# Halves of the values turned between WIV's last pieces, and two relations' counts in one number

## The reference, cut to what matters

```python
# layer 0: attention with two projections in a row for q, k and v
h = relu(layernorm(x))
q, k, v = h @ wq.T + bq, h @ wk.T + bk, h @ wv.T + bv
q2, k2, v2 = q @ wiq.T + biq, k @ wik.T + bik, v @ wiv.T + biv    # 16 heads of 64
scores = q2 @ k2.T / 8 + mask            # mask (96 x 96) from edges and types
x = x + (softmax(scores) @ v2) @ wo.T + bo
# layer 1: relational graph convolution over 1632 edges with 8 relations, and a gate
h = relu(layernorm(x))
u = h @ root + bias
for r in range(8):
    u += (sum of h[src] over the edges of relation r into dst / max(count, 1)) @ weight[r]
z = concat([u, h]) @ w_gate + b_gate
x = x + tanh(u) * z + h * (1 - z)
```

## Time and profile before

| | |
|---|---|
| median of 3 timed runs | 236.71 us (235.92 to 236.77) |
| profiled execution, its own time | 233.02 us |
| its span | 231.5 us |
| TensorE busy | 221.9 us, 96% |
| VectorE busy | 74.7 us, 32% |
| ScalarE busy | 20.1 us, 9% |
| GpSimd busy | 16.2 us, 7% |
| weights read by DMA | 72 fetches of 1024 KB; the queue's packets took 84.3% of 16 engines' span |
| granted TensorE clock | 1.000 over the span |

### The profile page before, as it was taken

One profiled execution on the slowest core, in us unless ns is written; L12 is line 12 of the kernel. 1 busy time (PEld: TensorE's weight loads), 2 busy tenths in 40 slices (PEclk: granted clock), 3 DMA queues, 4 the chain that ended last, 5 costly groups with the idle time before them and its releaser, 6 DMA issues.

```text
span 231.5 us, 10022 instructions
## 1 busy us (share of the span) xinstructions
PE 221.9 (96%) x4829; PEld 213.7 (92%) x4829; DVE 74.7 (32%) x134; ACT 20.1 (9%) x35; POOL 16.2 (7%) x42
## 2 busy tenths in 40 slices
PE   2999999999999999999999999999999999999993
PEld 2889989999999989889998999999999999999993
DVE  2469645231782130525875510000000000000624
ACT  2632000000110120131100000000000000000101
POOL 3260007600000000000000000000000000000000
PEclk9999999999999999999999999999999999999999
DMA  6999999999899866938887779999999998999302
GB/s 230 392 390 420 423 419 420 405 408 396 365 331 392 282 282 218 396 130 335 249 324 238 282 270 395 403 385 384 348 398 395 422 418 337 377 413 396 161 3 71
DMA packets 11275, 77.00 MB, mean 333 GB/s; under 512 B 1466, under 2 KB 1730, under 8 KB 2020
## 3 DMA queue, kind: packets, MB, share of 16 engines
q1 hardware_dynamic: 10704, 75.94, 84.3%
q10 hardware_dynamic: 532, 0.42, 0.6%
HBM read 75.97 MB, written 0.39 MB: 330 GB/s over the span
## 4 chain that ended last, share of the span: by engine, by line
PE 95%; DMA 2%; DVE 1%; issue 1%; ACT 0%
PE acc L728 80%; PE acc L986 3%; PE side L778 2%; PE turn L931 2%; DMA x_sb<-in_x 2%; PE side L931 1%; PE side L986 1%; PE turn L746 1%; PE turn L813 1%; DVE stats L469 1%; PE turn L829 0%; PE side L790 0%; PE side L797 0%; PE turn L790 0%; PE turn L797 0%
## 5 line engine op out<-in xcount | busy, mean ns | idle before, releaser
L728 PE MATMUL acc<-mean,raw 128*64 128x96 f32 x2048 | 85.4, 246 | 0.2
L728 PEld LDWEIGHTS acc<-mean,raw 128*64 128x64 f32 x2048 | 84.8, 137 | 0.9 <-issue 0.8
L728 PE MATMUL acc<-hT,raw 128*64 128x96 f32 x1024 | 44.8, 247 | 0.5 <-issue 0.5
L728 PEld LDWEIGHTS acc<-hT,raw 128*64 128x64 f32 x1024 | 43.1, 137 | 1.9 <-issue 1.5
L691 DVE TENSOR_TENSOR uT<-acc,uT 128x384 f32<-128x384 f32 x2 | 1.1, 558 | 81.9 <-PE acc L728 81.9
L728 PE MATMUL acc<-qT,raw 128*64 128x96 f32 x512 | 22.5, 247 | 0.7 <-issue 0.7
L728 PEld LDWEIGHTS acc<-qT,raw 128*64 128x64 f32 x512 | 21.6, 137 | 1.3 <-issue 1.1
L728 PE MATMUL acc<-kT,raw 128*64 128x96 f32 x512 | 22.3, 247 | 0.0
L728 PEld LDWEIGHTS acc<-kT,raw 128*64 128x64 f32 x512 | 21.4, 137 | 0.8 <-issue 0.7
L728 PE MATMUL acc<-uT,raw 128*64 128x96 f32 x256 | 12.2, 261 | 0.0
L728 PEld LDWEIGHTS acc<-uT,raw 128*64 128x64 f32 x256 | 11.8, 148 | 0.3 <-ACT uT L371 0.2
(11 more groups left out here) (170 smaller groups left out, 149.6 us busy)
## 6 DMA issues: line engine op xcount, KB each, us to landing
raw<-in_weights SPq DMA_DIRECT2D x72, 1024.0 KB, 6.6
x_sb<-in_x ACTq DMA_DIRECT2D x1, 192.0 KB, 3.7
x_sb<-in_x SPq DMA_DIRECT2D x1, 192.0 KB, 3.5
out<-out_rows SPq DMA_DIRECT2D x1, 192.0 KB, 2.1
out<-out_rows ACTq DMA_DIRECT2D x1, 144.0 KB, 2.5
out<-out_rows SPq DMA_DIRECT2D x1, 48.0 KB, 2.2
bias_rows<-in_biases ACTq DMA_DIRECT2D x1, 36.0 KB
edge_i<-in_edge_columns ACTq DMA_DIRECT2D x1, 25.5 KB
```

The lines of the kernel that those rows point to most:

```text
L728: mm = pe.matmul(a[g * HD:(g + 1) * HD, b, c * N:(c + 1) * N], raw[:, s, at:at + HD], moving(k0 + k), start=opens and k0 == 0 and c == 0 a ...
```

## The change

- WIV alone takes its pieces in the order KINDS_WIV = [0, 1, 2, 3]: output half 0 is done after the second piece, half 1 after the fourth. The wait for the second half of qT moves from the third piece to the second.
- `turn_v2(0)` stands between WIV's third and fourth piece, `mix_values(0)` and then `turn_v2(1)` behind the fourth. The transposes go to `acc[0]`, no longer to `turn`; the wait for the second turned half of the attention moves to `mix_values(0)`. ScalarE's order follows: take_v2(0), take_mix(0), take_v2(1), take_mix(1).
- `rel_hot` has 384 columns in place of 768: relations r and r + 4 share a column, and an edge of the upper four counts 2048 instead of 1 (there are 1632 edges). `rel_one_hot` gets a second operation, the multiplication by that step. `count(c)` is one instruction of 384 columns into bank 0 of `side`. No count stands before WO any more: 3 stand between the averages, 13 after them.
- VectorE splits the sums after the sum of squares: it copies them as int32 to `packed`, masks the low 11 bits, and subtracts to get the high part; ScalarE turns both into `counts`, the second with scale 1/2048.
- GpSimd computes the step of each edge and type modulo 4 in three more instructions of 102 x 16, ahead of the ones for the attention's codes. The iota and its copy are half as wide.

The diff, cut to its core:

```diff
+KINDS_WIV = [0, 1, 2, 3]
+PACK = 2048
+def kind_of(n):
+    return (KINDS_WIV if SEQUENCE[n // PIECES] == WIV else KINDS)[n % PIECES]
...
         def done_at(m, b):
-            return first_piece(m) + 3 + b
+            return first_piece(m) + (2 + 2 * b if m == WIV else 3 + b)
...
-            gp.iota(iota_i, [[1, R * N]], base=0, channel_multiplier=0).then_inc(iota_made, 1)
+            gp.iota(iota_i, [[1, TW]], base=0, channel_multiplier=0).then_inc(iota_made, 1)
...
-            step(gp.tensor_scalar(dup_f, type8_f, float(N), None, ALU.mult))
+            step(gp.tensor_scalar(upper_f, type8_f, float(R // 2), float(R // 2), ALU.is_ge, ALU.mult))
+            gp.tensor_scalar(rel_step_f, upper_f, (PACK - 1) / (R // 2), 1.0, ALU.mult, ALU.add).then_inc(edges_ready, 1)
+            step(gp.tensor_tensor(dup_f, type8_f, upper_f, ALU.subtract))
+            step(gp.tensor_scalar(dup_f, dup_f, float(N), None, ALU.mult))
...
-                act.activation(cols(v2, b)[0:N, :], turn[0:N, b, :], ACT.Copy).then_inc(v2_ready, 1)
+                act.activation(cols(v2, b)[0:N, :], acc[0][0:N, b, :], ACT.Copy).then_inc(v2_ready, 1)
...
             take_v2(0)
+            take_mix(0)
             take_v2(1)
-            take_mix(0)
             take_mix(1)
...
-            act.wait_ge(counted, EC)
-            for b in range(2):
-                act.activation(half(counts, b), side[0:N, b, 0:TW], ACT.Copy).then_inc(counts_taken, 1)
+            act.wait_ge(counts_split, 1)
+            act.activation(half(counts, 0), packed_low[:, :], ACT.Copy).then_inc(counts_taken, 1)
+            act.wait_ge(counts_split, 2)
+            act.activation(half(counts, 1), packed_high[:, :], ACT.Copy, scale=1.0 / PACK).then_inc(counts_taken, 1)
...
-                dve.tensor_scalar(rel_hot[:, c, :], node_iota[:, :], rel_key_f[:, c:c + 1], None,
-                                  ALU.is_equal).then_inc(rel_hot_ready, 1)
+                dve.tensor_scalar(rel_hot[:, c, :], node_iota[:, :], rel_key_f[:, c:c + 1], rel_step_f[:, c:c + 1],
+                                  ALU.is_equal, ALU.mult).then_inc(rel_hot_ready, 1)
...
             sum_chunks(3, squareT, squares_summed)
+            dve.wait_ge(counted, EC)
+            step(dve.tensor_copy(packed[:, :], side[0:N, 0, 0:TW]))
+            dve.tensor_scalar(packed_low[:, :], packed[:, :], PACK - 1, None, ALU.bitwise_and).then_inc(counts_split, 1)
+            dve.wait_ge(counts_split, 1)
+            dve.tensor_tensor(packed_high[:, :], packed[:, :], packed_low[:, :], ALU.subtract).then_inc(counts_split, 1)
             dve.wait_ge(var_shown, 1)
...
-                for b in range(2):
-                    mm = pe.matmul(side[0:N, b, 0:TW], src_hot[:, c, :], rel_hot[:, c, b * TW:(b + 1) * TW],
-                                   start=c == 0, stop=c == EC - 1)
-                mm.then_inc(counted, 1)
+                pe.matmul(side[0:N, 0, 0:TW], src_hot[:, c, :], rel_hot[:, c, :], start=c == 0,
+                          stop=c == EC - 1).then_inc(counted, 1)
...
             def turn_v2(b):
                 pe.wait_ge(taken, taken_at(WIV, b))
-                if b == 0:
-                    pe.wait_ge(attn_taken, 2)
-                turn_columns(turn, b, kT, v2_turned)
+                turn_columns(acc[0], b, kT, v2_turned)
             def mix_values(h):
                 pe.wait_ge(v2_ready, h + 1)
+                if h == 0:
+                    pe.wait_ge(attn_taken, 2)
...
             piece(n, of(qT), acc[1])
+            pe.wait_ge(taken, taken_at(WV, 1))
             piece(n + 1, of(qT), acc[1])
             turn_attn(0)
             turn_attn(1)
-            pe.wait_ge(taken, taken_at(WV, 1))
             piece(n + 2, of(qT), acc[1])
+            turn_v2(0)
             piece(n + 3, of(qT), acc[1])
-
-            turn_v2(0)
-            for c in range(0, 3):
-                count(c)
+            mix_values(0)
             turn_v2(1)
-            mix_values(0)
-            for c in range(3, 5):
-                count(c)
...
             average(turn[:, 0, 0:N], 0, True, False)
-            count(5)
+            for c in range(3):
+                count(c)
             pe.wait_ge(chunks_summed, 2)
             average(turn[:, 0, 0:N], 2, False, True).then_inc(mean_shown, 1)
-            for c in range(6, EC):
+            for c in range(3, EC):
                 count(c)
```

More of the change, by code:

```diff
@@ L58, in gnn_kernel @@
     assert weights.shape[0] == N_PIECES
+    assert E < PACK and R == 8
     with ExitStack() as ctx:
@@ L98, in gnn_kernel @@
         per_count = sb("per_count", [P, R * N])
+        packed = sb("packed", [N, TW], I32)
+        packed_low = sb("packed_low", [N, TW], I32)
+        packed_high = sb("packed_high", [N, TW], I32)
         bias_rows = sb("bias_rows", [NB * C, P])
@@ L113, in gnn_kernel @@
         edge_f = sb("edge_f", [EP, 4 * EC])
-        edge_tmp = sb("edge_tmp", [EP, 6 * EC])
+        edge_tmp = sb("edge_tmp", [EP, 8 * EC])
         key_mul = sb("key_mul", [2, EP], F16)
-        node_iota = sb("node_iota", [EP, R * N], F16)
+        node_iota = sb("node_iota", [EP, TW], F16)
         src_hot = sb("src_hot", [EP, EC, N], F16)
@@ L130, in gnn_kernel @@
         row_h = out_rows[0:2, :].bitcast(F16)[:, 0:E]
-        iota_i = per_count[0:EP, :].bitcast(I32)
+        iota_i = per_count[0:EP, 0:TW].bitcast(I32)
         same_key = v2[0:EP, :].bitcast(F16)[:, 0:EC * EP].rearrange("p (c e) -> p c e", e=EP)
-        rel_hot = mean[0:EP, :, :].rearrange("p c n -> p (c n)").bitcast(F16)[:, 0:EC * R * N]\
-            .rearrange("p (e n) -> p e n", n=R * N)
+        rel_hot = mean[0:EP, :, :].rearrange("p c n -> p (c n)").bitcast(F16)[:, 0:EC * TW]\
+            .rearrange("p (e n) -> p e n", n=TW)
         acc = [ctx.enter_context(nc.psum_tensor(f"acc{i}", [P, 2, HALF], F32)) for i in range(2)]
@@ L184, in gnn_kernel @@
         counted = sem("counted")
+        counts_split = sem("counts_split")
         counts_taken = sem("counts_taken")
@@ L232, in gnn_kernel @@
         src_f, dst_f, type5_f, type8_f = (edges(k) for k in range(4))
-        tmp = [edge_tmp[:, k * EC:(k + 1) * EC] for k in range(6)]
-        key_f, rel_key_f, code_e, base_f, dup_f, zero_f = tmp
+        tmp = [edge_tmp[:, k * EC:(k + 1) * EC] for k in range(8)]
+        key_f, rel_key_f, code_e, base_f, dup_f, zero_f, rel_step_f, upper_f = tmp
         def first_piece(m):
@@ L273, in fetch @@
             def fetch(n):
-                where = PIECES * SEQUENCE[n // PIECES] + KINDS[n % PIECES]
+                where = PIECES * SEQUENCE[n // PIECES] + kind_of(n)
                 if n >= SLOTS:
@@ L555, in _ @@
             dve.tensor_tensor(tw[:, 12:16], tw[:, 0:4], tw[:, 8:12], ALU.add).then_inc(type_w_ready, 1)
-            dve.wait_ge(edges_ready, 3)
+            dve.wait_ge(edges_ready, 4)
             for c in range(EC // 2):
@@ L719, in piece @@
             def piece(n, moving, a, opens=True, closes=True):
-                s, kind = n % SLOTS, KINDS[n % PIECES]
+                s, kind = n % SLOTS, kind_of(n)
                 b, k0 = kind // 2, CH * (kind % 2)
```

## The result

Over 20 timed runs each, the changed kernel has a median of 233.77 us (229.81 to 237.76) and the kernel before 235.26 (232.31 to 236.77). All ratios and their 95% intervals, and the medians called quick, leave out executions over 1.5% above the fastest of the same kernel. The ratio is 0.9895, interval 0.9853 to 0.9937: 1.1% faster, as forecast. The changed kernel's 8 quick executions have a median of 230.5 us; its other 12 reach 237.8, and the one that was profiled (236.98 us, span 235.2) is among them.

A forecast was written before the change was run, and what follows sets the result against it. The prediction took TensorE as the bound: 1.50 us saved between WIV and WO plus 1.18 between WO and ROOT make 2.68, so 236.71 - 2.7 = 234.0 us, 1.1% faster. The range was 232.9 to 235.3 us.

The forecast's parts named there:

- TensorE's list sets the time: Whole kernel: TensorE, on 95% of the chain of waits, is the bound; what leaves its list, 2.68 us, leaves the time.
- Place 1: TensorE's list between WIV and WO: 2.08 us, first turn included, instead of 3.58, so 1.50 us less.
- X: The end of WIV's last piece on TensorE; WO was forecast to start 1.51 us after it.
- The mix: TensorE's mix between WIV and WO: starts at once after WIV's last piece and takes 0.81 us.
- The hand-over: From the mix's end over ScalarE's copy to WO: forecast at 0.70 us.
- the margin of 0.03: Between WIV and WO: VectorE frees the second turn at X + 0.78, just under the mix's end at X + 0.81.
- Place 2: TensorE's list between WO and ROOT: 20 counts behind the second average become 13, 1.18 us less.
- The three counts between the averages: TensorE between WO and ROOT: three counts take 0.51 us, no difference from two counts plus a rest.
- The split: VectorE behind the sum of squares: 1.6 us, between 0.9 and 1.8, with 1.0 us of slack, nothing on the path.
- The early part: GpSimd's three more instructions and the one-hots: masking delayed by about 0.7 us against 5.2 of slack, cost zero.
- The level: Whole time: the saving is carried over to the median as it is, 236.71 - 2.7 = 234.0 us.
- Rival A: In the relations the weight stream takes the saving back: time stays at 236.7 us, or half, 235.4; chance 0.09.

The follow-up runs named there:

- e2: The changed kernel with every weight fetch after the first six halved: 227.15 us.
- e3: The changed kernel with halved weight fetches after the first six and WIV's part of the change undone, leaving the packed counts: 227.43 us.
- e1: The kernel before with every weight fetch after the first six halved: 229.55 us, ratio 0.9795 to the kernel before.
- e15: The changed kernel with halved weight fetches after the first six and the split's copy out of PSUM done five times: 228.52 us.
- e9: The changed kernel with 8 slots and each of the 16 products of show_codes done three times: 241.01 us, one execution.
- e10 to e12: The changed kernel with at most two weight fetches under way, 235.73 us; at most three, 233.86 us; each fetch made as two of half the columns, 244.46 us.
- e13: The changed kernel with products 128 output columns wide in place of two of 64, except in WG_U: 288.61 us.
- e5: The changed kernel itself, unchanged, run again beside the kernel before: 231.28 us, ratio 0.9851.
- e6: The changed kernel with 8 slots in the ring of weights in place of 6: 236.63 us, ratio 1.0002 to the kernel before.

## Why the prediction was right or wrong

**TensorE's list sets the time: right.** With the stream thinned, the stretch of the change is 2.62 us shorter (forecast 2.68), and the ratio of the full kernels, 0.9895, is 2.45 us of 233 (by its interval 1.5 to 3.4).

**Place 1: right, by terms that partly cancel.** Forecast 2.08 us for the first turn and the way from X to WO, measured 0.57 + 1.30 = 1.87 in e2. The mix took 0.66, not 0.81: behind a piece it takes 0.66, as the second mix did before, and behind a turn 0.81. The hand-over took 0.64. The forecast put it at 0.70, the way to WO's weight load, and subtracted from 3.58, which ends with WO's first product; to the product its rows give 0.78, and its sum would have been 1.42 less instead of 1.50. These errors partly cancel. On the other side, WIV's last two pieces took 2 x 2.79 instead of 5.43: taking them apart for the first turn costs 0.15, which the forecast had as 0. The second turn did wait for VectorE (0.19 on its weight load), the margin of 0.03 not being enough; it didn't matter, because the mix's copy gates WO.

**Place 2: right.** 4.43 became 3.34 in e2, 1.09 less (forecast 1.18). The three counts between the averages took 0.62, where the forecast had 0.51, and cost 0.05 more than the two of before.

**What makes the gain.** The forecast gave 1.50 us to place 1, where both parts of the change meet, and never asked what each is worth. The runs part it: by the stretch packing gives 2.50, the new order 0.12 beside it and -0.10 alone. The whole times agree within their scatter (e3 is 2.12 us under e1, e2 another 0.28).

**The split: right.** 1.45 us of instructions and 1.5 with its waits (forecast 1.6), slack to its reader 1.5 less the hand-over (forecast 1.0); e15 shows it from the other side.

**The early part: no cost, but two prices were off.** The one-hots of half the width took no less: eight in 2.85 us (2.72 in the earlier trace rows), inside the forecast's bounds. GpSimd's masking started at 17.34, 1.5 us later, twice the delay expected, and took 3.06 us instead of 1.66; VectorE's one-hot that ran beside it from 18.80 took 3.21 where its like took 1.75 before. The masking ended at 20.40, its reader came at 22.98.

**The level: wrong.** The step that failed is "the median of the runs stands 3.7 us above the profiled execution, and no row tells where; I carry the saving over as it is". 236.71 was the median of three runs that were all high, 235.92 to 236.77: of the kernel before's 20 executions 12 lie between 232.31 and 235.75, and the profiled 233.02 is of their kind. From 233.02 the forecast had 230.3, and the quick executions give 230.5; what was put on record, 234.0 with a low end of 232.9, lies above them. The median of all 20, 233.77, is inside the range, since 12 of them took 233.4 us and more; nothing in the forecast's working says so, and it is luck.

**Where those microseconds are.** Rival A had put them down to TensorE waiting for weights. It is half right: halving the stream takes some 4.8 us off the kernel before, and both spreads shrink. But the gaps are not in front of pieces; they come 128 products apart, move with the list (e9), and end 1.1 to 1.6 us after a packet of instructions has. TensorE waits for instructions while the stream loads the DMA engines. Of the 5.5 us between the two profiled executions of the changed kernel, spans 235.2 and 229.7, 3.5 are such idling in the rows of products (6.4 us against 2.9), and 1.1 are WQ's first piece, of 5.03 and 3.93 us, which isn't explained. The rows for it stood in the chain of the kernel before, three idle times on TensorE before 45 us, which the forecast doesn't name:

```profile
29.27 0.50 issue
...
35.61 0.41 issue
36.01 5.50 PE acc L728 x128
41.51 0.24 issue
```

With the full stream the packets start later. That they stand behind weights in an engine's queue is only argued: e10 to e12, meant to shorten that wait, did not gain, and why eight slots do worse than six is open. The test with fewer instructions at the same stream, e13, had a slower TensorE and stays open.

## What to carry to other kernels

Take the base of a forecast from the profiled execution that the durations come from, and ask of a median that stands apart whether three runs can bear it. Where an idle time is put down to nothing, count the instructions between two of them before naming a cause: a period that is the same in instructions and falls in the middle of a tile is not data. Then look up when the packets of the instruction queue end, and whether the engine goes on a fixed time later. Where the chain runs through a fetch, see in the engine's own timeline whether it idled. On a TensorE-bound path, work that covers a hand-over is only worth its cover, so halving it pays until the hand-over shows.

## What the runs showed of the hardware

- TensorE's idle times of 0.2 to 2.1 us stand 128 products with their weight loads apart, or a multiple of it; instruction packets are 16 KB, one per 5.6 to 6.1 us (79 us, 14 and 13 packets), and the product behind a stop starts 1.1 to 1.6 us after one ends.
- With half the weight bytes (201 GB/s from 42 to 60 us, DMA share 0.63, in e1) there are no such idle times; at 407 to 419 GB/s in the same window (e5, e6) there are. The rate and the share of busy time alone don't tell: in that window the kernel before has none, at 403 GB/s and a share of 1.00, and from 131 to 160 us e5 has none, at 378 GB/s and a share of 0.97.
- More slots in the ring made the kernels slower: 238.6 against 234.4 us before, 234.4 against 231.1 after (quick medians).
- Weights fetched as twice as many transfers, with rows of 4 KiB instead of 8 and the same bytes, took a ratio of 1.0416 where the changed kernel has 0.9851 to 0.9895: 12 to 13 us.
- A float32 product of 96 columns with 128 x 128 weights takes 112 ns; two with 128 x 64, into the two halves of the output, take 83 together.
- VectorE's comparison with a second operation and a second scalar per partition took 0.36 us for 384 float16 columns, where 768 with one operation took 0.34. GpSimd's instruction of 96 x 96 beside it took 0.64 us, and 2.88 beside the wider one.
